# A two-layer graph network on one core: 36 batches of 31 sorted and 14 plain tiles in place of 34 of 31 and 16, and a rewritten prologue

## The reference

```python
h = jnp.maximum(_layernorm(x), 0.0)
# layer 0 (edge features of 16 columns)
msg = jax.nn.relu(h[src] + edge_attr_16 @ W_edge.T + b_edge)
agg = jax.ops.segment_sum(msg, dst, num_segments=6250)
h = (h + agg) @ W1.T + b1
h = relu(gamma * (h - mean) * rsqrt(var + 1e-5) + beta)    # over the nodes
x = x + h @ W2.T + b2
h = jnp.maximum(_layernorm(x), 0.0)
# layer 1 (edge features of 64 columns)
Y = jax.nn.relu(concat([h[src], edge_attr_64]) @ M_W.T + M_b)
Z = jax.ops.segment_sum(Y, dst, num_segments=6250)
x = x + jax.nn.relu(concat([h, Z]) @ U_W.T + U_b)
```

## Time and profile before

| | before |
|---|---|
| median of three runs | 4677.96 us |
| the profiled execution's own time | 4683.23 us |
| its span | 4681.4 us |
| mean granted TensorE clock | 0.676 of full speed |
| busy, share of the span | PE 55%, PE weight loads 45%, POOL 44%, DVE 32%, ACT 21% |
| instructions | PE 25733 matmuls, DVE 2605, ACT 2153, POOL 2185 |
| moved by DMA | 567.79 MB, 121 GB/s on average |
| chain that ended last | 13% of the span "another core or an unknown queue", PE 7%, DVE 3%, issue 3% |

### The profile page before, as it was taken

How to read it: one execution, slowest core, us unless ns; L and a number is a source line. 1 busy time by engine, 2 the same in 40 slices (tenths; PEclk the granted TensorE clock), 3 DMA queues, 4 the chain that set the end, 5 groups by cost and what they waited for, 6 DMA issues and landing times. The chain is left out here.

```text
span 4681.4 us, 73575 instructions
## 1 busy us (share of the span) xinstructions
PE 2556.5 (55%) x25733; PEld 2127.0 (45%) x25733; DVE 1516.7 (32%) x2605; ACT 960.6 (21%) x2153; POOL 2080.6 (44%) x2185
## 2 busy tenths in 40 slices
PE   3465555554555555655456555555655555555554
PEld 3354445543454444544345444454544444444443
DVE  4332223322232222322223222322444334433443
ACT  1321112221122111222122121222321111111111
POOL 5344544445434454344544454354243443344343
PEclk9766666666666666666667666666666766766676
DMA  6554434543345443454445443443345544554451
GB/s 188 138 140 126 116 106 127 151 118 111 107 130 144 114 113 105 132 145 117 111 116 139 132 119 108 127 122 82 93 120 133 127 115 113 132 128 115 113 137 45
DMA packets 707916, 567.79 MB, mean 121 GB/s; under 512 B 495308, under 2 KB 609216, under 8 KB 703224
## 3 DMA queue, kind: packets, MB, share of 16 engines
q1 hardware_dynamic: 628632, 403.50, 33.2%
q0 software_dynamic: 69440, 107.94, 8.6%
q10 hardware_dynamic: 9632, 53.14, 3.0%
HBM read 296.20 MB, written 268.18 MB: 121 GB/s over the span
## 5 line engine op out<-in xcount | busy, mean ns | idle before, releaser
L1200 PE MATMUL ps_w<-arena 128*64 128x128 f32 (+1 forms) x9040 | 1217.6, 313 | 997.7 <-issue 891.3
L737 POOL DMA_INDIRECT edge_store<-side,slot_idx x1054 | 1016.1, 964 | 1551.0 <-issue 1260.5
L759 POOL DMA_INDIRECT gathered_rows<-node_table_l,plain_slot x1116 | 1056.7, 947 | 956.8 <-DVE arena L1623 577.5
L1200 PEld LDWEIGHTS ps_w<-arena 128*64 128x64 f32 x9040 | 917.3, 166 | 1210.6 <-issue 1092.3
L1600 DVE TENSOR_TENSOR arena<-ps_c,dst_rel 128x1024 f32<-128x1024 f32 (+1 forms) x476 | 526.1, 1105 | 1083.2 <-remote 822.4
L1135 PE MATMUL ps_p<-w_both,side 80*128 80x128 f32 x3228 | 643.6, 360 | 392.4 <-issue 133.1
L912 ACT ACTIVATE arena<-arena 128x512 f32<-128x512 f32 (+1 forms) x616 | 366.2, 595 | 2228.6 <-remote 859.7
L1135 PEld LDWEIGHTS ps_p<-w_both,side 80*128 80x128 f32 x3228 | 560.9, 261 | 434.9 <-issue 264.4
L1585 DVE TENSOR_SCALAR arena<-arena,iota_p 125x512 bf16<-125x512 bf16 (+1 forms) x442 | 146.7, 350 | 1083.4 <-ACT arena L899 765.2
L1188 PE MATMUL ps_r<-tab,arena 125*128 125x64 bf16 x5100 | 284.5, 212 | 360.5 <-DVE arena L1585 251.7
L1609 DVE TENSOR_TENSOR arena<-ps_r,arena 128x512 f32<-128x512 f32 (+1 forms) x476 | 299.3, 629 | 504.7 <-remote 485.9
(11 more groups left out here) (124 smaller groups left out, 1022.6 us busy)
## 6 DMA issues: line engine op xcount, KB each, us to landing
edge_store<-zeros SPq DMA_DIRECT2D x34, 3300.0 KB
arena<-edge_store SPq DMA_DIRECT2D x34, 1650.0 KB, 10.7
src_store<-arena SPq DMA_DIRECT2D x204, 256.0 KB
side<-attr SPq DMA_DIRECT2D x172, 256.0 KB
arena<-edge_store SPq DMA_DIRECT2D x34, 1056.0 KB
arena<-edge_store SPq DMA_DIRECT2D x34, 594.0 KB
plain_store<-plain_e SPq DMA_DIRECT2D x35, 512.0 KB
side<-plain_store SPq DMA_DIRECT2D x35, 512.0 KB
```

Source lines behind the costliest of these rows:

```text
L737: pool.indirect_dma_start(out=store, in_=stage[:, c, i, :], in_offset=None, out_offset=bass.IndirectOffsetOnAxis(ap=slot_idx[:, s, t + i:t ...
L759: pool.indirect_dma_start(out=rows[s][:, i, :], out_offset=None, in_=table[layer], in_offset=bass.IndirectOffsetOnAxis(ap=plain_slot[:, s, ...
L1200: mm = pe.matmul(ps_sum[layer][t % 2][:, 0:width], msg[:, slot, t, :], dst_match[:, slot, t, 0:width], start=(first and t <= layer), stop= ...
```

## The change

- `PLAIN` goes from 16 to 14, so a batch has 45 tiles, and there are 36 batches, all alike; the last has 31 sorted tiles and 6 plain ones with edges. `NB` and `PARTS` are both 36 and `LAST_PREPARED` is 32. `last_plain` is called once a layer instead of twice. Plain windows are 64 wide instead of 72.
- A plain batch is now a unit of 8 tiles and one of 6 (8 and 8 before); the fourth chunk has two tiles.
- ACT's prologue copies transposed features and chunks c0 to c3 of batch 2 inside the steps 5 to 9 of its loop; PE projects c0 after the transposes of group 0 and c1 to c3 after those of groups 4, 5 and 6, instead of after groups 0 to 3. The transposed features have another place in SBUF, apart from what `load_edges` fills.
- SP's prologue: the fill of batch 3's store goes ahead of the stores of the node table; the loads of the sorted edges of batches 0 and 1 stand together, and the attribute loads of batch 3 and the store of `acc` come between the stores of batch 0's matrices.

```diff
-PLAIN = 16
+PLAIN = 14
-TILES = 1645
+TILES = 1620
-NB = BATCHES - 1
+NB = BATCHES
-PLAIN_WINDOW = 72
+PLAIN_WINDOW = 64
...
             fill(2, 0)
             for quarter in range(2):
                 load_first(2, quarter)
+            sp.wait_ge(filled[1], 16)
+            fill(3, 1)
             store_nodes(0)
             for quarter in range(2, NQ):
                 load_first(2, quarter)
-            sp.wait_ge(filled[1], 16)
-            fill(3, 1)
...
-            group_landed(0)
-            load_edges(0, 0)
-            keep_acc(0)
-            for q in range(2):
-                sp.wait_ge(projected, FIRST_LOADS // NQ * len(CHUNKS) + 2 * (q - 1))
-                load_attr(AHEAD, *QUARTERS[q], q)
-            group_landed(1)
-            load_edges(1, 1)
+            for g in range(2):
+                group_landed(g)
+                load_edges(g, g)
             for u in range(NU):
                 store_src(0, 0, u)
+                if u in (1, 2):
+                    sp.wait_ge(projected, FIRST_LOADS // NQ * len(CHUNKS) + 2 * (u - 2))
+                    load_attr(AHEAD, *QUARTERS[u - 1], u - 1)
+                if u == 3:
+                    keep_acc(0)
...
@@ ACT, prologue
-            for g in range(NG):
-                copy_turned(0, g)
-                if g < 4:
-                    evacuate(2, 0, g)
+
+                for g in {5: (0, 1), 6: (2, 3), 7: (4,), 8: (5,), 9: (6,)}.get(step, ()):
+                    copy_turned(0, g)
+                    for c in {0: (0,), 4: (1,), 5: (2,), 6: (3,)}.get(g, ()):
+                        evacuate(2, 0, c)
...
@@ PE, prologue
             for g in range(NG):
                 turn(0, g)
-                if g < 4:
-                    project_first(2, 0, g)
+
+                if g in (0, 4, 5, 6):
+                    project_first(2, 0, (0, 4, 5, 6).index(g))
...
@@ ACT, PE and DVE, each layer
-            for m in range(NB - 1, PARTS):
-                last_plain(0, m)
+            last_plain(0, NB - 1)
             last_windows(0)
```

More of the change, by code:

```diff
@@ L67 @@
 FIRST_LOADS = AHEAD * NQ
[L68 removed]
+LAST_TILES = -(-EDGES // P) - (NB - 1) * BATCH - BUCKET
 GENERAL = (BATCH + 1) // 2
@@ L1082, in _ @@
             more = general_flag(act)
-            for m in range(NB - 1, PARTS):
-                last_plain(1, m)
+            last_plain(1, NB - 1)
             last_windows(1)
```

64 lines of the change are left out of this document (29 added, 35 removed).

## The result

The changed kernel takes 4744.75 us, the median of four runs (4736.43 to 4751.9), against 4679.36 us before (median of four runs beside it): a ratio of 1.0131, 95% interval 1.0098 to 1.0165. The profiled execution took 4751.9 us, its span is 4750.1 us. The forecast was 4698 us and a range up to 4720. The direction was right; the forecast rise of 20 us is less than a third of the 65 us measured.

What follows compares the result with a forecast made beforehand. The bound was taken as POOL's indirect-DMA bursts plus the other engines' time in the gaps. Terms of +100, -38, -52, +9 and 0 gave +20 us with decimals kept, so 4698 us, range 4650 to 4720.

Steps and rivals of the forecast that it cites:

- What bounds the kernel: Whole kernel: a turn is POOL's time plus the others' time; 59.1 us of DMAs and 37.5 idle in layer 0.
- PE almost stands still while POOL issues: Beside POOL's bursts: 208 matmuls in 72 us with bursts, against 256 in 26 us without.
- solid bursts: POOL's timeline: indirect DMAs run in solid bursts with idle time between, such as a 7.05 us gap in layer 0.
- Layer 0, the loop: Layer 0's turns: 32 of 93.65 us in place of 30 of 96.55, +100 us.
- the turn becomes 96.55 - 2.5 - 0.4: A layer 0 turn: two gathers fewer take off 2.5 us, shorter plain work 0.4, giving 93.65 us.
- Layer 0, the end: From the last sorted batch's first scatter to DVE's last sum: fewer gathers and no third set, -38 us.
- Layer 1, the loop: Layer 1's periods: 35 of 33.44 us in place of 34 of 35.94, -52 us.
- Layer 1, the end: From layer 1's last burst start to the last sum: 35.4 us in place of 26.4, +9 us.
- Prologue: Before the loop: an earlier batch 2 start is eaten by gaps between its pieces; 0, bounds -12 and +6 us.
- The prologue gives what it can: Rival: POOL starts batch 2 at 122 us and isn't stopped; -10 to -12 us, 4687 us, chance 0.20.
- The gaps shrink by more: Rival: a layer 0 turn loses 1.9 instead of 0.4 us; 48 us less, 4650 us, chance 0.20.
- The gathers are hidden: Rival: PE works beside bursts, turns keep 96.55 and 35.94 us; about +216 us, 4894 us, chance 0.03.

Runs made afterwards that it cites:

- e11: Kernel before with 14 instead of 16 gathers a batch in layer 0 (last two plain tiles' source rows left out), slow kind: 4630.1 us, ratio 0.9887.
- e10: Changed kernel, POOL waiting before layer 0's gathers until ACT has copied plain chunk c1 of the batch before, slow kind: 4541.8 us, 0.9698 of before.
- e17: Changed kernel with the stop for c1, plus a stop in layer 1 between its 8 and 6 gathers, slow kind: 4416.8 us, 0.9440 of before.
- e13: Changed kernel, POOL waiting before layer 0's gathers for plain chunk c3 in place of c1, slow kind: 4673.3 us, 0.9973 of before.
- e9: New batches alone: the changed kernel with the prologue of before, slow kind: 4742.5 us, 1.0139 of before.
- e12: Kernel before with the new prologue and the stop for c1 before layer 0's gathers, slow kind: 4543.3 us, 0.9701 of before.
- e7: Changed kernel, POOL waiting before layer 0's gathers until ACT has copied plain chunk c1 of the batch before, fast kind: 2837.4 us, 0.9769 of before.
- e19: Changed kernel with stops for c1 and in layer 1, plus stops before c2, c6 and between layer 0's gathers, slow kind: 4398.8 us, 0.9369 of before.
- e15: Changed kernel with the stop for c1, plus a stop in layer 1 between its 8 and 6 gathers, fast kind: 2993.5 us, 1.0309 of before.

## Why the prediction was wrong, point by point

- **What bounds the kernel.** Right in the main: on the slow kind a turn is POOL's time plus the others' time, and the gap is released 4 to 5 us after the burst. Wrong in "PE almost stands still while POOL issues": it stands from 4 to 10 us into a burst on. The earlier trace rows averaged over 72 us in which two such starts lie; windows of 8 us show them. Wrong also in "solid bursts": the very turn of the earlier trace rows has a later stop of 1.70 us. The Trainium skill, page "SBUF — State Buffer", section "SBUF: two separate sides", lets PE and ACT wait on nobody. The fast kind agrees with that rule (286 matmuls in 28 us under a full stream). On the slow kind PE is held up (36 in 28.5 us); that it waits at a port of SBUF, of which the rule speaks, isn't shown.
- **Layer 0, the loop: the step that failed.** The step is "the turn becomes 96.55 - 2.5 - 0.4". It took one mean turn and subtracted from it. The long turns fell by 2.6, but the mean of before held ten turns of 93.7 us that depended on a stop of POOL, and none of them came back. It cost 1.74 us a turn, 56 us of the 156: 1.4 us for the ten short turns lost, 0.3 for the long ones. e11 showed that shorter bursts alone do it, e10 and e17 that a stop is what makes the difference. Both sorts stood in the trace of before: its turns are 91.7 to 100 us long. The later stop in the turn of the earlier trace rows, in POOL's timeline of before:

```profile
1838.21 0.96 POOL L737 DMA_INDIRECT edge_store<-side,slot_idx  x1 [1.70 <-issue]
```

- **Layer 0, the end**: -41 for -38, right.
- **Layer 1, the loop**: -33 for -52, mis-sized. Before, most periods had a gap of 15.7 or 16.6 us, and five of 34 bursts a short stop of 1.86 us with a gap of 14.3 behind it; now the gap is 16.9 in most. The idle time of POOL grew by 0.5 us a period, where I had put nothing and 0.5 as the bound. The loss of the short stops doesn't explain it: e11 has the layer 1 of before, no such stop in it, and the same period (35.92 against 35.94 us). The same layer 1 as in the changed kernel takes 33.31 us a period in e13, so 33.97 isn't fixed by the program alone; what sets it is open.
- **Layer 1, the end**: +3.4 for +9, right in sign, 6 us too much.
- **Prologue**: 0 was forecast, bounds -12 and +6; measured -18. Of it 7 us are there with the old prologue too (e9's first scatter of batch 3 is at 238.9), and come from the shorter gathers and gaps before it; the new order gives 11, and in e12 with the batches of before 14 (232.1 against 245.8): at its bound of -12 or just beyond. The feared gaps between the pieces of batch 2 were 1.9 and 3.6 us and not 4 to 5. In the whole kernel it can't be seen on the slow kind: the changed kernel and e9 are both at 4742 to 4745 us, on different chips, since e9's turns are 94.66 us on average. Whether the new prologue has a part in that is open. On the fast kind it is worth 17 to 22 us.
- **Rivals.** None came out as a whole. "The prologue gives what it can" happened in the prologue: POOL starts batch 2 at 121.4 us and is hardly stopped, but the loop outweighed it. "The gaps shrink by more" is out: the mean gap grew. "The gathers are hidden" is out on both kinds: on the fast one POOL is the bound and each gather counts most. The sign on a chip of the other kind was not among the cases at all. The chances given add up to 0.98.

The best kernel for both kinds is the changed one with the stop for c1 (e7, e10): 0.977 and 0.970 of before. On the slow kind alone e19 and e17 are better, 0.937 and 0.944, and on the fast one they lose 14% and 3%.

## What to carry to other kernels

Don't subtract from a mean turn before looking at its spread: where turns come in two sorts, ask what makes the short ones, and whether the change leaves that in place. Where one engine's burst holds up the others, count their progress in windows much shorter than the burst: if they lose little at its start, a short stop in it can give more than it costs, provided that it ends as soon as the first things behind it are done (4.9 us gained 6.2 a turn, 8.8 us only 1.9). And time a change on more than one chip: here the same two kernels stood at 1.013 on one and at 0.976 on another.

## What the runs showed of the hardware

- The same kernel takes 2903 to 2906 us on three chips and 4669 to 4694 us on four. Its granted clock is 0.81 on the first and 0.67 on the others. POOL's DMAs take the same time on both (a scatter of the changed kernel 972 ns on the fast kind, 966 on the slow). What differs is that on the slow kind PE, ACT and DVE together come nearly to a stand 4 to 10 us into a burst of indirect DMAs, and start again 2 to 5 us after its end or in a stop. What they wait for isn't in the trace ("issue", "remote"), and no run took it apart. It isn't DMA bandwidth by what the windows show (share 0.19, 46 GB/s in the stand of 28.5 us).
- A stop for the landed rows of 8 gathers in layer 1 lasts 4.85 us on the fast kind (e15) and 2.4 us on the slow one (e17). The traffic beside it differs: in one stop of e15 the DMA engines are full, at 323 GB/s, in one of e17 they move 15 GB/s. Whether the chip itself has a part in it isn't shown.

```profile
2604.90:2609.70 4.80, 4.80 (x102) 4.29 (x103) 4.77 (x8) 1.26 (x2) 0.00 (x0) 1.00 1.17 323
...
3599.97:3602.18 2.21, 1.39 (x13) 0.91 (x14) 0.27 (x1) 0.00 (x0) 0.01 (x1) 0.50 0.07 15
```
